# First stage of a state-space and expert kernel: the second batch is normalised earlier, the B product is computed by halves, and VectorE takes two du copies and four scalings

## What is computed

```python
h = _layernorm(x) * (1 + ca) + sa
# attn_ref: forward and backward state-space pass over h (DI=256 channels, DS=16 states)
xh, z = split(h @ in_proj.T)
xc = silu(conv_b + sum(xp[:, k:k+L] * conv_w[:, k] for k in range(4)))
dt, B, C = split(xc @ x_proj.T)
delta = softplus(dt @ dt_w.T + dt_b)
state = state * exp(delta * A) + (delta * xc) * B     # 1024 steps, 16 states
y = (sum over states of state * C + xc * D) * silu(z)
out = y @ out_proj.T                                  # both passes are added to h
x = x + ga * layernorm(h + yf + yb)
# then a second layernorm, top-64 routing to 8 experts, an MLP each, and a scatter-add
```

## Time and profile before

| | |
|---|---|
| three timed runs | 625.02 us median (620.01, 625.02, 630.39) |
| profiled execution | 622.88 us, of it span 621.1 us |
| granted TensorE clock over the span | 0.937 of full speed |
| busy PE, DVE, ACT, POOL | 503.3, 483.6, 445.4, 335.3 us |
| first scan (L904) starts at | 52.04 us |
| loads issued: packed weights; x of batch 1 | 1.84; 4.63 us |
| chain that ended last | PE 41%, ACT 27%, DVE 21%, issue 8% |

### The profile page before, as it was taken

How to read it: one execution, slowest core, us unless ns; L and a number is a source line. 1 busy time by engine, 2 the same in 40 slices (tenths; PEclk the granted TensorE clock), 3 DMA queues, 4 the chain that set the end, 5 groups by cost and what they waited for, 6 DMA issues and landing times.

```text
span 621.1 us, 9122 instructions
## 1 busy us (share of the span) xinstructions
PE 503.3 (81%) x3376; PEld 412.0 (66%) x3376; DVE 483.6 (78%) x642; ACT 445.4 (72%) x850; POOL 335.3 (54%) x155
## 2 busy tenths in 40 slices
PE   3486989986799999689998969698866568598897
PEld 3154855876688677577855757696755456398596
DVE  3775888977887777598799948989999997769522
ACT  2359876999988889899877899889777731155150
POOL 3013665867966676796665858677666681200000
PEclk9787998998999999799999999799989988768989
DMA  7030121211421212031221112222532213000101
GB/s 245 1 106 30 41 101 35 101 70 35 136 73 69 70 68 102 34 107 69 77 68 61 69 69 72 69 102 69 152 120 96 73 21 116 2 1 1 35 1 35
DMA packets 17884, 43.45 MB, mean 70 GB/s; under 512 B 1328, under 2 KB 7600, under 8 KB 17584
## 3 DMA queue, kind: packets, MB, share of 16 engines
q1 hardware_dynamic: 17840, 42.87, 20.8%
HBM read 41.56 MB, written 1.31 MB: 69 GB/s over the span
## 4 chain that ended last, share of the span: by engine, by line
PE 41%; ACT 27%; DVE 21%; issue 8%; POOL 1%; DMA 1%; POOLq 0%; DVEq 0%; ACTq 0%
ACT dBuT L555 13%; PE pro L1106 11%; PE yT L1106 9%; PE yT L1110 9%; PE dBu L1110 7%; DVE area L908 6%; ACT dA L548 6%; DVE area L904 4%; PE dBu L1106 4%; PE pro L1110 2%; DVE area L937 1%; DVE top L935 1%; DVE area L740 1%; ACT th L516 1%; ACT pre L523 1%
## 5 line engine op out<-in xcount | busy, mean ns | idle before, releaser
L465 POOL TENSOR_TENSOR hc<-area 128x1024 f32<-128x1024 f32 x127 | 306.2, 2413 | 153.5 <-DVE area L904 81.8
L555 ACT ACTIVATE dBuT<-area,bT 128x256 f32<-128x256 f32 x512 | 217.2, 500 | 42.2 <-PE dBu L1110 41.9
L1110 PE MATMUL dBu<-ident,dBuT 128*128 128x128 f32 x1024 | 148.7, 284 | 52.0 <-DVE area L908 29.0
L1110 PEld LDWEIGHTS dBu<-ident,dBuT 128*128 128x128 f32 x1024 | 119.3, 145 | 66.3 <-DVE area L908 35.3
L548 ACT ACTIVATE dA<-area,Aneg 128x1024 f32<-128x1024 f32 x128 | 146.2, 1143 | 3.5 <-DVE area L908 1.8
L1110 PE MATMUL yT<-ident,hc 128*128 128x128 f32 x1024 | 141.9, 285 | 0.0
L1110 PEld LDWEIGHTS yT<-ident,hc 128*128 128x128 f32 x1024 | 123.0, 147 | 18.2 <-issue 16.3
L908 DVE TENSOR_TENSOR_SCAN area<-dA,area,dBu 128x512 f32<-128x512 f32 x64 | 81.8, 1277 | 4.8
L904 DVE TENSOR_TENSOR_SCAN area<-dA,area,dBu 128x512 f32<-128x512 f32 x64 | 81.8, 1277 | 4.5 <-DVE area L904 0.5
L904 DVE TENSOR_TENSOR_SCAN area<-dA,dBu 128x512 f32<-128x512 f32 x64 | 77.1, 1204 | 10.1 <-PE dBu L1110 9.7
L908 DVE TENSOR_TENSOR_SCAN area<-dA,dBu 128x512 f32<-128x512 f32 x64 | 77.3, 1208 | 7.6 <-PE dBu L1110 6.8
(11 more groups left out here) (196 smaller groups left out, 583.0 us busy)
## 6 DMA issues: line engine op xcount, KB each, us to landing
area<-c_rows SPq DMA_DIRECT2D x64, 512.0 KB, 3.6
dBuT<-w_in SPq DMA_DIRECT2D x1, 2048.0 KB, 9.0
wp<-wpack_in SPq DMA_DIRECT2D x1, 1030.0 KB, 7.5
x<-x_in SPq DMA_DIRECT2D x2, 512.0 KB, 7.1
hc<-bcast_in SPq DMA_DIRECT2D x1, 1024.0 KB, 10.2
out<-x SPq DMA_DIRECT2D x4, 256.0 KB, 2.3
hT<-w_in SPq DMA_DIRECT2D x1, 512.0 KB, 8.1
acc<-w_in SPq DMA_DIRECT2D x1, 512.0 KB, 8.7
```

What stands on the lines that cost most here:

```text
L465: g_.tensor_tensor(hc[:, e % 3, :], hs[:, e % 3, :], Cb[:, g % 3, :], ALU.mult).then_inc(hc_done, 1)
L555: return nc.scalar.activation(dBuT[:, g % 2, n, :], duT[par][:, n, :], ACT.Copy, scale=bT[:, par, n, s:s + 1])
L1110: return nc.tensor.matmul(out, in_, ident[:, :] if idn is None else idn, start=start, stop=True, is_transpose=True, skip_group_check=True)
```

## The change

Batch 1 is loaded right after the packed weights, with a semaphore of its own. VectorE does the bias parts and the whole normalisation of batch 1 before the first taps; TensorE turns both after the gate product, the bias parts into the bank `pro`; ScalarE modulates batch 1 and writes bias3 before the two tanh. The gate rows and the tap weights are done by VectorE before BT. The B product is accumulated for both chunks over channel half 0 first, then over half 1, so that its first part waits for half 0 alone. DU 0 and 1 become DV 0 and 1, copied by VectorE. Of the eight dBuT blocks of the first state, ScalarE makes four, and VectorE the other four in `first_high_blocks`; TensorE waits for these before its second chunk.

```diff
--- before.py
+++ after.py
@@ -38,7 +38,7 @@
 FIRST_ITEMS = ([("B", 0), ("B", 1), ("BT", 0)]
-               + [("DT", j) for j in range(4)] + [("DU", j) for j in range(4)])
+               + [("DT", j) for j in range(4)] + [("DV", 0), ("DV", 1), ("DU", 2), ("DU", 3)])
 LAST_ITEMS = [("YT", j) for j in range(4)] + [("O", j) for j in range(2)]
 NORM_ITEMS = [("LT", 0), ("LT", 1), ("LG", 0), ("ST", 0), ("ST", 1), ("PT", 0)]
...
@@ -199,7 +199,7 @@
...
-        s_x = sem("x_loaded")
+        s_x = [sem(f"x{b}_loaded") for b in range(NB)]
         s_w = sem("weights_loaded")
         s_cw = sem("conv_rows_loaded")
...
@@ -369,17 +370,16 @@
...
         def _(sp):
             def load_x(b):
-                sp.dma_start(x[:, b], x_d[b].rearrange("(n p) d -> p n d", p=P)).then_inc(s_x, 16)
+                sp.dma_start(x[:, b], x_d[b].rearrange("(n p) d -> p n d", p=P)).then_inc(s_x[b], 16)
             load_x(0)
             sp.dma_start(modp, mod_d).then_inc(s_m, 16)
             sp.dma_start(wp[:, :], wpack_d).then_inc(s_w, 16)
+            load_x(1)
+            sp.dma_start(dtw[:, :, :], dtw_d).then_inc(s_v, 16)
             sp.dma_start(convrow, bcast_d[0:CONVW_COLS].partition_broadcast(P)).then_inc(s_cw, 16)
             sp.dma_start(lnv[:, :, :].rearrange("p a b -> p (a b)"),
                          bcast_d[CONVW_COLS:CONVW_COLS + 2 * D].partition_broadcast(P)).then_inc(s_v, 16)
-            sp.dma_start(dtw[:, :, :], dtw_d).then_inc(s_v, 16)
-            sp.wait_ge(s_x, 16)
-            load_x(1)
             for g in range(NG):
                 u, s = divmod(g, DS)
...
@@ -559,12 +559,15 @@
...
                 if g % DS == 0:
                     wait_item(act, "DU", 3, u)
+                if g == 0:
+                    wait_item(act, "DV", 1, 0)
+                if g % DS == 0:
                     wait_item(act, "BT", 0, u)
                 if g >= 2:
...
                 for n in ns:
                     last = scale_block(g, n)
-                if n == NBLK - 1:
+                if n == NBLK - 1 or g == 0:
                     last.then_inc(dbut_ready, 1)
...
@@ -577,18 +580,21 @@
...
                 nc.scalar.activation(xc[0][:, half, :], xh(half), ACT.Identity, bias=biasc[:, half:half + 1],
                                      scale=convc[:, 0, half, DC - 1:DC]).then_inc(acc0_ready, 1)
+            modulate(1)
+            act.wait_ge(parts_turned, 1)
+            nc.scalar.activation(bias3[:, :, :, :].rearrange("p d h c -> p (d h c)"), pro[0:3, :],
+                                 ACT.Copy).then_inc(bias_ready, 1)
             for half in range(NH):
                 act.wait_ge(taps_ready, half + 1)
...
             nc.scalar.preload_act_table(ACT.Softplus)
             for k, j in FIRST_ITEMS:
-                if (k, j) == ("DU", 0):
+                if (k, j) == ("DU", 2):
                     act.wait_ge(others_ready, 1)
                     exp_tile(0)
-                    modulate(1)
                 item_a(k, j, 0)
             low, high = range(NBLK // 2), range(NBLK // 2, NBLK)
-            scale_blocks(0, range(NBLK))
+            scale_blocks(0, low)
             scale_blocks(1, low)
             for e in range(NT):
...
@@ -694,7 +700,7 @@
...
                 rows = range(b * NBLK, (b + 1) * NBLK)
                 rs = slice(b * NBLK, (b + 1) * NBLK)
-                dve.wait_ge(s_x, 16 * (b + 1))
+                dve.wait_ge(s_x[b], 16)
                 for n in rows:
                     last = nc.vector.bn_stats(st[:, n, :], x[:, b, n % NBLK, :])
...
@@ -757,6 +763,7 @@
...
             def bias_parts():
+                dve.wait_ge(scaled_ready, 1)
                 step(nc.vector.tensor_copy(part32[:, :, 0], part16[:, 0, :]))
                 step(nc.vector.tensor_tensor(part32[:, :, 2], biasc, part32[:, :, 0], ALU.subtract))
...
@@ -764,6 +771,19 @@
...
                                         ALU.subtract).then_inc(parts_ready, 1)
+            def keep_gate_rows():
+                dve.wait_ge(gab_ready, 1)
+                nc.vector.tensor_copy(gtemp[:, 0, :], dBu[0][:, 0:NB * D]).then_inc(gab_kept, 1)
+
+            def first_high_blocks():
+
+                wait_item(dve, "BT", 0, 0)
+                wait_item(dve, "DV", 1, 0)
+                wait_item(dve, "DU", 3, 0)
+                for n in range(NBLK // 2, NBLK):
+                    last = nc.vector.tensor_scalar(dBuT[:, 0, n, :], duT[0][:, n, :], bT[:, 0, n, 0:1], None, ALU.mult)
+                last.then_inc(high0_ready, 1)
+
             def tap_weights():
...
@@ -772,9 +792,6 @@
...
                                                               ALU.mult, ALU.mult)
                 last.then_inc(weights_ready, 1)
-                dve.wait_ge(parts_turned, 1)
-                nc.vector.tensor_copy(bias3[:, :, :, :].rearrange("p d h c -> p (d h c)"),
-                                      dBu[1][0:3, :]).then_inc(bias_ready, 1)
             def other_weights():
...
@@ -825,6 +842,10 @@
...
                     nc.vector.scalar_tensor_tensor(gz[par][:, 2 * j:2 * j + 2, :].rearrange("p n d -> p (n d)"),
                                                    th[:, :], 1.0, src, ALU.add, ALU.mult).then_inc(item_dve, 1)
+                elif kind == "DV":
+                    dve.wait_ge(pro_ready, NUMBER[it] + 1)
+                    nc.vector.tensor_copy(duT[par][:, c * BPC:(c + 1) * BPC, half * P:(half + 1) * P],
+                                          src.rearrange("p (n d) -> p n d", n=BPC)).then_inc(item_dve, 1)
                 elif kind == "BT":
                     dve.wait_ge(pro_ready, NUMBER[it] + 1)
...
@@ -980,21 +1001,23 @@
...
                     nc.vector.tensor_tensor(x[:, b, ns, :], yT[:, 0, ns, :], x[:, b, ns, :], ALU.add).then_inc(x2_ready, 1)
+            bias_parts()
+            x_stats(1)
+            x_norm(1)
             first_taps(0)
             first_taps(1)
...
             first_x(1)
             other_weights()
-            x_stats(1)
-            x_norm(1)
+            dve.wait_ge(xn_turned, 2)
+            keep_gate_rows()
+            tap_weights()
             item_v("BT", 0, 0)
             for half in range(NH):
                 first_du(half)
-            bias_parts()
-            tap_weights()
-            dve.wait_ge(gab_ready, 1)
-            dve.wait_ge(xn_turned, 2)
-            nc.vector.tensor_copy(gtemp[:, 0, :], dBu[0][:, 0:NB * D]).then_inc(gab_kept, 1)
+            item_v("DV", 0, 0)
+            item_v("DV", 1, 0)
+            first_high_blocks()
             for e in range(NT):
                 g, half = divmod(e, NH)
...
@@ -1138,8 +1161,9 @@
...
             def turn_parts():
                 pe.wait_ge(parts_ready, 1)
+                pe.wait_ge(modt_ready, 1)
                 for k in range(NBIAS):
-                    last = turn(dBu[1][0:3, k * P:(k + 1) * P], part32[:, k, :], True)
+                    last = turn(pro[0:3, k * P:(k + 1) * P], part32[:, k, :], True)
                 last.then_inc(parts_turned, 1)
...
@@ -1165,7 +1189,9 @@
...
                     last = mm(dst[:, part * DI:(part + 1) * DI], hT[:, b, at:at + P], wz[:, dr, :], True, True)
                 elif kind == "B":
-                    if part == 0:
+                    if u == 0:
+                        wait_x(pe, part, j, u)
+                    elif part == 0:
                         for h in range(NH):
                             wait_x(pe, h, j, u)
...
@@ -1232,6 +1258,8 @@
...
                 if half == 0 and i == 0:
                     pe.wait_ge(dbut_ready, g + 1)
+                if e == 0 and i == 1:
+                    pe.wait_ge(high0_ready, 1)
                 if q >= 3:
                     pe.wait_ge(scan_done, q - 2)
...
@@ -1259,16 +1287,18 @@
...
                 last.then_inc(yacc_done, 1)
-            for k, j in FIRST_ITEMS:
+            turn_parts()
+            turn_xn(1)
+            pe.wait_ge(bias_ready, 1)
+            for part in range(NH):
+                for j in range(NCH):
+                    item_t(("B", j, 0), part)
+            for k, j in FIRST_ITEMS[NCH:]:
                 if (k, j) == ("DT", 0):
                     pe.wait_ge(s_v, 32)
-                if (k, j) == ("DU", 0):
-                    turn_xn(1)
                 for part in range(parts_of(k)):
                     item_t((k, j, 0), part)
             pe.wait_ge(ht_ready, 2)
-            turn_parts()
-            pe.wait_ge(bias_ready, 1)
             pe.wait_ge(weights_ready, 1)
             pe.wait_ge(others_ready, 1)
...
```

More of the change, by code:

```diff
@@ L99 @@
 BY_ACT = ("B", "DT", "DU", "YT", "LT")
-BY_DVE = ("X", "Z", "BT", "O", "LG", "ST", "PT")
+BY_DVE = ("DV", "X", "Z", "BT", "O", "LG", "ST", "PT")
 def count_of(it, kinds):
@@ L226, in build_block @@
         scaled_ready = sem("scaled_bias_ready")
+        high0_ready = sem("first_high_blocks_ready")
         others_ready = sem("other_weights_ready")
@@ L512, in item_a @@
                 half, c = divmod(j, NCH)
```

(4 more changed lines are left out.)

## The result

| | before | changed |
|---|---|---|
| timed runs, median | 626.55 us (620.01 to 630.39, 4 runs) | 614.65 us (613.43 to 619.32, 4 runs) |
| ratio of the times | | 0.9882, 95% interval 0.9836 to 0.9928 |
| profiled execution, its span | 622.88, 621.1 us | 614.09, 612.1 us |
| first scan | 52.04 | 45.90 |
| first scan to the routing scan of batch 1 (L945, now L966) | 521.21 | 521.33 |

What follows compares the result with a forecast made beforehand. The prediction took ScalarE's queue before the scan loop and TensorE's B product as the bound. Terms 1.21 + 1.33 + 0.95 + 1.60 = 5.1 us turn 623.95 into 618.9, forecast as 619 us, range 613 to 626.

Steps and rivals of the forecast that it cites:

- normalisation in the hole: Batch 1's normalisation in VectorE's idle time before the first tap: ends at 19.25 us, tap at 19.96, price zero.
- x of batch 1: Load before the normalisation: lands at an estimated 11 to 12 us; upper bound 14.9, making everything from the first tap 1.4 later.
- tanh behind modulation and bias copy: ScalarE before the first tanh: tanh ends at 26.8 us, wanted by VectorE at 27.62, so hidden by 0.8.
- B by halves: TensorE's B product starts once half 0 of xc is ready, at 28.98 instead of 30.19: 1.21 us gained.
- length of B: B product on TensorE: same length taken; if the clock rose at 34.3 regardless, a gain of 0.5 instead of 1.2.
- modulation away: Batch 1's modulation leaves ScalarE's queue behind the first dA: 1.33 us gained.
- two du copies: Two of four DU copies leave ScalarE's queue before the blocks, 0.48 us each: 0.95 us gained.
- four blocks: Four of the first state's eight block scalings leave ScalarE, 0.40 us each: 1.60 us gained.
- first turns to first scan: Entry of the scan loop: first turns move from 50.85 to 45.75 us, first scan from 52.04 to 46.9.
- BT came only at 37.51: VectorE after the taps: moving the normalisation away gives nothing by itself there, as its next work, BT, came only at 37.51.
- Rival C: Loop loses the gain through TensorE's clock: slower than before below mean 0.917, 627 us at 0.90; chance 0.13.
- D: Rival that TensorE's clock turns out higher instead: 0.96 takes 5.9 us off, giving 612; chance 0.13.

Runs made afterwards that it cites:

- (5), x1_last: Changed kernel with the loads in the old order, x of batch 1 last after a wait for batch 0's: 616.14 us, ratio 0.9880 to the kernel before.
- (4), norm_late: Changed kernel with the normalisation of batch 1 back behind the tanh multiplications: 618.10 us, ratio 0.9930 to the kernel before.
- (3), act_du: Changed kernel with all four du copies on ScalarE again: 620.51 us, ratio 0.9929 to the kernel before.
- (2), act_blocks: Changed kernel with all eight blocks of the first state scaled by ScalarE, profiled twice: 621.80 us, ratio 0.9978 to the kernel before.
- experiment 1, b_whole: Changed kernel with B computed item by item again, the halves undone: median 618.46 us, ratio 0.9909 to the kernel before.
- experiments 2 and 7: 2: changed kernel, all eight blocks on ScalarE, 621.80 us. 7: changed kernel and kernel before run once more, unedited, 615.46 us and 629.03 us.
- warm: Changed kernel with filler turns of the identity (36, 4 and 18) on TensorE: median 615.87 us, ratio 0.9881 to the kernel before.
- warm_more: Changed kernel with the TensorE filler turns, plus DU 2 copied and a fourth block scaled by VectorE: 617.04 us, ratio 0.9914 to the kernel before.
- more_dve: Changed kernel with DU 2 also copied and a fourth-state-block scaling also done by VectorE, starting at block 3: 614.99 us, ratio 0.9872 to the kernel before.
- only_halves: Kernel before with B by halves and nothing else: median 623.02 us, ratio 0.9995 to the kernel before.
- (8): Changed kernel with DU 2 also copied by VectorE and its block scalings beginning at block 3: 614.99 us, ratio 0.9872 to the kernel before.

## Why the prediction was right

Step by step, in the profiled execution:

| step | predicted | measured |
|---|---|---|
| normalisation in the hole | 0, ends 19.25 | ends 19.12, first tap at 19.89 |
| x of batch 1 | 11 to 12, at most 14.9 | no wait at 12.70; 14.9 in the old order, 1.34 us (5) |
| tanh behind modulation and bias copy | 0, 0.8 to spare | 0, 2.6 to spare, 1.2 of it from a projection that ended earlier |
| B by halves | 1.21 | 1.28 by its start, 0.07 of it because all before it ran 0.07 earlier |
| length of B | unchanged | 5.71 to 5.22, 0.49 more |
| modulation away | 1.33 | 1.33 (4) |
| two du copies | 0.95 | 0.97 (3) |
| four blocks | 1.60 | 1.59 (2) |
| first turns to first scan | unchanged | 0.46 more |
| loop | unchanged | 0.12 longer |
| rest | unchanged | 2.98 shorter |

The path was read rightly: four terms, three of ScalarE's queue and one of TensorE's, while the pieces that were moved into VectorE's and ScalarE's holes cost nothing. The numbers in brackets are the experiments that undid each. The sum of the terms, 5.1, became 6.14 at the first scan, and the missing 1.0 is one thing twice.

First, the granted clock rose 3.2 us after B's start instead of 4.1, so B was 0.49 shorter; the prediction named an end for B of 34.7, and it was 34.1. As far as the runs show this is luck: in the twelve profiled executions without fillers the rise came 3.0 to 6.1 us after B's start, and in the two of the kernel before at 4.1 and 6.1. With B by halves it came at 3.0 to 4.7 in nine executions, with B in one piece at 4.1 to 6.1 in three; whether the order of B's products has a part in it is not shown.

Second, the first turns of dBuT still found the clock up, having idled 2.84 us instead of 4.77, which gave 0.46. This goes with the change, since a shorter queue on ScalarE leaves a shorter gap: with gaps of 2.22 to 2.84 us the first turns ran at full speed in four executions, with gaps of 3.18 to 4.77 at half speed in seven (in experiment 1 the clock was low before the gap). The prediction had taken the turns to be unchanged.

One reading was wrong without cost. The prediction says that BT came only at 37.51, so that taking the normalisation away there gives nothing. But BT's turns ended at 36.57 + 0.69 = 37.26, and it was for VectorE's own normalisation, up to 35.45 + 2.13 = 37.58, that BT waited. It cost nothing all the same, because du waited another 2.15 us for softplus. Likewise VectorE's two copies, for which no row was at hand, took 1.28 us where two of 0.67 were taken.

By the Trainium skill (TensorE: Matmul & The Clock Gate, What you observe) the transition moves by some 0.5 us from run to run, and by the estimate made from that the term would be 1.0 to 1.5. The start and the length of B together gave 1.8, and the rise moved by 2.0 us between the two executions of the kernel before: more than the page says, and the measurement decides.

The rest, 2.98 us, was not in the sum. It is TensorE's clock, as rivals C and D had it, and on D's side. The last part of the changed kernel's profile ran at a granted clock of 1.00, before's at 0.96:

```profile
567.23:612.10 44.87, 38.49 (x298) 33.74 (x296) 18.86 (x38) 12.50 (x40) 0.00 (x0) 1.00 0.09 24
```

```profile
573.25:621.10 47.85, 41.52 (x309) 36.78 (x308) 18.86 (x38) 12.53 (x40) 0.00 (x0) 0.96 0.08 23
```

VectorE and ScalarE were busy for the same time in both. In experiments 2 and 7 the rest took 50.21, 49.72 and 49.77 us at 0.90, 0.91 and 0.91, so the order is the same in all five. Rival C priced 0.02 of mean clock at 5.1 us, so 0.016 at 4.1; past the first scan 2.9 were measured.

The times themselves can be held apart by their granted clock. At 0.953 the kernel before took 618.4 to 618.9 us (11 of the 64 single times taken beside the experiments, one of 1220.2 left out) and the changed kernel 613.4 to 614.3 (5 of 10): 4.5 us between the middles, near the forecast 5.1. Against the changed kernel's 614.1 stand 615.2 with B in one piece (4 of 10, +1.1), 615.0 and 615.6 with the old load order, and 615.0 with the du copies on ScalarE (one, at 0.955); the halves alone gave 617.4 (one of 10, -1.2). So an estimate from these times is that 4.5 of the ratio's 7.4 us is work taken off the path, and that the other 3 goes with the clock. An equal mean does not show that the clock was low at the same places.

What stays open is whether that other part is the change's too. The runs point to it in two ways and do not settle it. The fall of the clock between B and du, worth 1.9 and 2.2 us at the last softplus, came in two of three profiled executions with B in one piece, and in none of nine with halves and without fillers. And the last part took 44.7 to 44.9 us in all five executions of the changed kernel, warm, warm_more and more_dve and in three variants (b_whole, norm_late, x1_last), but 47.8 to 50.2 in the other six (before twice, only_halves, act_du and act_blocks twice). The time of the first scan does not order the whole times: with blocks on ScalarE it is 2.0 to 2.8 late and the median 7 us, and none of that kernel's eleven times had a clock above 0.945; with halves alone it is 2.4 early and the median unmoved.

## What to carry to other kernels

Sum the terms of a first stage on the engine whose timeline has no idle time in front of the loop. Every piece removed from that queue was worth its spacing in the rows, to 0.03 us, until the next engine became the path: after that 0.9 us of removed work gave 0.4 (8). A piece moved into another engine's hole is free as long as its input lands in time, and moving the load with it is part of the change (1.34 us here). For a change of a few microseconds in 600, the median of a few times is a poor judge: read the start of the loop in the trace, compare times of equal granted clock, and hold the granted clock of each stretch beside any difference where no instruction changed.

## What the runs showed of the hardware

Work on TensorE alone held the clock up in one execution: with 36 turns of the identity in the gap, B took 3.6 us instead of 5.2. In a second, with the same fillers, the clock fell while they ran, at 25.5, and came back to 1.00 at 29.0 us, with nothing but fillers running. The 1.9 us gained at the loop's entry were lost again in the loop, which took 3.6 us more, with a lower granted clock at places where the program was unchanged. One program in two executions, the kernel before, differed by 2.9 us at the first scan, 1.2 in the loop and 1.9 in the last part, with a mean granted clock of 0.929 and 0.937.
